# A four-layer RWKV block, two FP4 feed-forward passes and one attention pass on one core: a division seeded from the squared denominator, roots prepared on VectorE, pieces of the normalisations moved to GpSimd, and the FFN weights rounded at the start

## The reference, cut to what matters

```python
y = rwkv(layernorm(x))                  # 4 layers, below
x = x + y
x = x + fp4_ffn(layernorm(x))           # gate, up: 352 columns; silu(gate) * up; down
x = x + causal_attention(layernorm(x))  # inner width 64
x = x + fp4_ffn(layernorm(x))           # the same FFN weights again

# one rwkv layer
h = layernorm(x)*w1 + b1;  hh = h shifted by one token
k, v, r = (h*tm + hh*(1-tm)) @ W.T      # three mixes, three matrices
# scan over tokens with a running maximum pp:
out_t = (e1*aa + e2*v_t) / (e1*bb + e2)
x = x + (sigmoid(r) * out) @ Wo.T
h = layernorm(x)*w2 + b2
kf = square(relu(mix(h) @ Wck.T));  x = x + sigmoid(mix(h) @ Wcr.T) * (kf @ Wcv.T)
```

## Time and profile before

| | us |
|---|---|
| median of 3 runs | 1373.24 (1371.58 to 1373.82) |
| the profiled execution | 1373.36 |
| its span, from first to last instruction | 1372.0 |

### The profile page before, as it was taken

The page is one execution under the profiler, slowest core; times in us unless marked ns, Lnnn a source line. Parts: engine busy times, 40 slices in busy tenths (PEclk is TensorE's granted clock), DMA queues, the critical chain, the costliest instruction groups (busy, mean ns, idle before and its releaser), DMA issues.

```text
span 1372.0 us, 23396 instructions
## 1 busy us (share of the span) xinstructions
PE 1274.4 (93%) x7177; PEld 918.9 (67%) x7177; DVE 1247.3 (91%) x2157; ACT 1238.0 (90%) x2411; POOL 1184.9 (86%) x1413
## 2 busy tenths in 40 slices
PE   3589999999999999999999899998999998999997
PEld 1246666766766766766776567765677786677776
DVE  5889999999999999999999999669999577988995
ACT  5689999999999999999999799877787899999875
POOL 6788999999999999999999999969998556765784
PEclk9789999999999999999999999999999999999999
DMA  7000000001000000000000000100000000000011
GB/s 236 1 0 2 1 1 1 2 1 33 1 1 1 1 1 1 1 1 1 1 1 1 1 2 8 32 23 25 23 1 1 1 1 1 1 16 17 24 31 39
DMA packets 26924, 18.54 MB, mean 14 GB/s; under 512 B 1072, under 2 KB 26160, under 8 KB 26800
## 3 DMA queue, kind: packets, MB, share of 16 engines
q1 hardware_dynamic: 26800, 17.05, 4.2%
HBM read 12.85 MB, written 4.19 MB: 12 GB/s over the span
## 4 chain that ended last, share of the span: by engine, by line
ACT 32%; PE 26%; POOL 17%; issue 14%; DVE 11%; DMA 0%; ACTq 0%; SPq 0%; POOLq 0%; DVEq 0%
ACT z L793 6%; PE ps L1265 4%; ACT kf L913 4%; ACT kf L906 4%; PE ps L1237 3%; PE ps L1244 3%; PE ps L1315 3%; ACT past L898 3%; ACT h L840 2%; POOL W L740 2%; PE ps L1253 2%; PE ps L1297 2%; POOL W L746 2%; PE ps L1080 1%; ACT rc L878 1%
## 5 line engine op out<-in xcount | busy, mean ns | idle before, releaser
L1206 PEld LDWEIGHTS ps<-W,kf 128*128 128x128 f32 x2048 | 248.3, 192 | 58.6 <-issue 58.4
L1188 PE MATMUL ps<-xk,W 128*128 128x512 f32 x512 | 253.6, 598 | 0.8 <-ACT kf L906 0.8
L1206 PE MATMUL ps<-W,kf 128*128 128x128 f32 x2048 | 248.6, 275 | 0.0
L906 ACT ACTIVATE kf<-ps 128x512 f32<-128x512 f32 x256 | 147.1, 599 | 5.4 <-PE ps L1188 5.4
L1080 PEld LDWEIGHTS ps<-idn,z 128*128 128x128 f32 x664 | 78.8, 143 | 104.0 <-issue 53.7
L1080 PE MATMUL ps<-idn,z 128*128 128x128 f32 x664 | 104.6, 281 | 44.7 <-POOL z L651 18.5
L793 ACT ACTIVATE z<-X,ln_rs 128x128 f32<-128x128 f32 x320 | 137.9, 502 | 2.7 <-POOL ln_rs L613 2.6
L913 ACT ACTIVATE kf<-kf 128x1024 f32<-128x1024 f32 x128 | 136.2, 1065 | 0.0
L746 POOL TENSOR_TENSOR W<-W,hsc 128x704 f32<-128x704 f32 x64 | 88.8, 1388 | 47.0 <-DVE W L503 46.8
L1188 PEld LDWEIGHTS ps<-xk,W 128*128 128x128 f32 x512 | 87.1, 192 | 62.4 <-issue 53.9
L611 POOL TENSOR_TENSOR ln_rs<-ln_rs,mhalf 128x8 f32<-128x8 f32 (+1 forms) x70 | 111.1, 1587 | 0.0
(11 more groups left out here) (182 smaller groups left out, 3841.8 us busy)
## 6 DMA issues: line engine op xcount, KB each, us to landing
X<-x_in SPq DMA_DIRECT2D x16, 256.0 KB, 6.6
xi<-x_in SPq DMA_DIRECT2D x16, 256.0 KB, 2.9
out<-X SPq DMA_DIRECT2D x16, 256.0 KB, 2.3
W<-weights SPq DMA_DIRECT2D x4, 832.0 KB, 8.3
W<-fp4w SPq DMA_DIRECT2D x1, 560.0 KB, 3.7
row<-rows SPq DMA_DIRECT2D x1, 192.0 KB, 3.0
wqkv<-qkv SPq DMA_DIRECT2D x1, 96.0 KB, 6.1
idn<-ident SPq DMA_DIRECT2D x1, 64.0 KB, 3.2
```

Of the source, the lines that this page charges most:

```text
L906: e.activation(kf[r % 3][:, f, :], (pF0, pF1)[f % 2][:, :], ACT.Relu).then_inc(relu_done[f], 1)
L1188: e.matmul((pF0, pF1)[f % 2][:, :], w_of(r, WCK + f), xk[r % 2][:, :], start=True, stop=True).then_inc(kf_mm[f], 1)
L1206: last = e.matmul(chunk(pKV, j), kf[r % 3][:, f, j * 128:(j + 1) * 128], w_of(r, WCV + f), start=f == 0 and j == 0, stop=f == 3, skip_grou ...
```

## The change

The division: the seed is now computed from den squared (one more ACT operation, `Square`, into `rc`, and a wait of ACT on itself, `den2_done`), with half the slope. The end is one square and one DVE operation in place of two; `mul_u` is gone, and signs and constants are folded into `WO`.

`w` is added to d already in `sub_d` (one DVE operation as before, of another kind), so that both `Relu` of `args` and the clip need no bias tile; the constants of the clip are adapted.

`rsqrts` on POOL keeps the power and the product. The two operations before it are made by DVE in a new step `variances`, on the same 128x8 tiles.

Norm 1 is now 2 + 2 pieces, norm 2 is 1 + 3 (ACT + POOL): POOL does 5 of 8 where it did 3 of 8.

The FFN weights are loaded right after the fourth tile of x, into the space of layer 1, and rounded in ticks 1 to 5; PE transposes them in ticks 10 to 12, in three steps, ACT copies them in ticks 7 to 9, and the attention matrices are folded at the start. SP issues the loads of layers 1 to 3 behind a wait for the last transposition; `PREPARE_AT` moves DVE's scaling of those layers to ticks 12, 18 and 26.

All four order lists are rewritten, with other offsets.

```diff
-SEED = LN2 * (127.0 - 0.04367744889921346)
-CUBIC, LEAD = 0.9991106956842978, 1.000889996847986
+SEED = LN2 * 0.5 * (127.0 - 0.048852061236122075)
+VERTEX, REST, LEAD = 1.4972871244454433, 0.7471212163971999, 1.0056154043227372
...
+            def variances(s):
+                if 0 <= s < NR + LN2_LAG:
...
+                    e.tensor_scalar(rs[:, 1, :], st[:, :, 1], -1.0, None, ALU.mult)
+                    e.tensor_scalar(rs[:, 2, :], st[:, :, 2], 1.0 / 128.0, EPS, ALU.mult, ALU.add).then_inc(ready, 1)
...
             def sub_d(r):
-                    e.tensor_tensor(dd[r % 2][:, :], pK[:, :], pp[r % 2][:, 0:T], ALU.subtract).then_inc(d_done, 1)
+                    e.scalar_tensor_tensor(out=dd[r % 2][:, :], in0=pK[:, :], scalar=col(ew, r), in1=pp[r % 2][:, 0:T],
+                                           op0=ALU.add, op1=ALU.subtract).then_inc(d_done, 1)
...
-            def mul_u(r):
-                if 0 <= r < NR:
-                    w.wait_ge(sq1_done, r + 1)
-                    w.wait_ge(ps_done, r + 1)
-                    e.scalar_tensor_tensor(out=pO[:, :], in0=pO[:, :], scalar=CUBIC, in1=p[r % 2][:, :],
-                                           op0=ALU.add, op1=ALU.mult).then_inc(u_done, 1)
...
             def rwkv(r):
-                    w.wait_ge(u_done, r + 1)
-                    e.scalar_tensor_tensor(out=rc[r % 2][:, :], in0=er[r % 2][:, :], scalar=2.0, in1=pO[:, :],
-                                           op0=ALU.subtract, op1=ALU.mult).then_inc(rwkv_done, 1)
+                    w.wait_ge(sq1_done, r + 1)
+                    w.wait_ge(ps_done, r + 1)
+                    e.scalar_tensor_tensor(out=rc[r % 2][:, :], in0=pO[:, :], scalar=REST, in1=p[r % 2][:, :],
+                                           op0=ALU.add, op1=ALU.mult).then_inc(rwkv_done, 1)
...
             def rsqrts(s):
-                    roots(n_1.rs2[s % 3][:, :, lo:hi], n_1.st2[s % 3][:, lo:hi, :], n_1.nr)
+                    w.wait_ge(ready, s + 1)
+                    e.tensor_tensor(rs[:, 0, :], rs[:, 2, :], mhalf[:, 0:hi - lo], ALU.pow).then_inc(*own.next())
+                    w.wait_ge(*own.so_far())
+                    e.tensor_tensor(rs[:, 1, :], rs[:, 1, :], rs[:, 0, :], ALU.mult).then_inc(n_1.nr, 1)
...
-                    e.activation(ed[r % 2][:, 0, :], dd[r % 2][:, :], ACT.Relu, bias=col(ew, r))
-                    e.activation(ed[r % 2][:, 1, :], dd[r % 2][:, :], ACT.Relu, bias=col(wneg, r), scale=-1.0).then_inc(args_done, 1)
+                    e.activation(ed[r % 2][:, 0, :], dd[r % 2][:, :], ACT.Relu)
+                    e.activation(ed[r % 2][:, 1, :], dd[r % 2][:, :], ACT.Relu, scale=-1.0).then_inc(args_done, 1)
...
             def seeds(r):
                 if 0 <= r < NR:
                     w.wait_ge(wo_mm, r - 1)
                     w.wait_ge(den_done, r + 1)
-                    e.activation(rc[r % 2][:, :], er[r % 2][:, :].bitcast(I32), ACT.Exp, bias=SEED,
-                                 scale=-LN2 / 2.0 ** 23).then_inc(seed_done, 1)
+                    e.activation(rc[r % 2][:, :], er[r % 2][:, :], ACT.Square).then_inc(den2_done, 1)
+                    w.wait_ge(den2_done, r + 1)
+                    e.activation(rc[r % 2][:, :], rc[r % 2][:, :].bitcast(I32), ACT.Exp, bias=SEED,
+                                 scale=-LN2 / 2.0 ** 24).then_inc(seed_done, 1)
...
+                if b == 3:
+                    e.dma_start(qw, fp4w).then_inc(fp4_here, 16)
+            w.wait_ge(q_turned, 3)
+            for l in range(1, L):
+                e.dma_start(W[:, l, :], weights[:, l, :]).then_inc(w_here[l], 16)
```

More of the change, by code:

```diff
@@ L570, in vector @@
-                a_bn(att_job(t - 1))
-                f_bn(ffn_job(t + 2))
-                scan_pp(t - 4)
                 a_inverse(att_job(t - 5))
-                a_add(att_job(t - 6))
-                mul_u(t - 6)
-                fx_add(ffn_job(t - 2))
+                rwkv(t - 6)
+                sub_d(t - 4)
                 mul_up(ffn_job(t - 4), 0)
                 mul_up(ffn_job(t - 4), 1)
+                bn2(t - 7)
                 fx_sub(ffn_job(t - 2))
+                fx_scale(ffn_job(t - 1))
@@ L580, in vector @@
+                fh_add(ffn_job(t - 5), 0)
+                mix_k(t - 8)
+                mix_r(t - 8)
+                mul_up(ffn_job(t - 4), 2)
                 gated(t - 5)
-                sub_d(t - 4)
-                fh_add(ffn_job(t - 5), 0)
-                mul_up(ffn_job(t - 4), 2)
-                rwkv(t - 6)
                 fh_sub(ffn_job(t - 5), 0)
-                fx_scale(ffn_job(t - 1))
                 mul_up(ffn_job(t - 4), 3)
-                bn2(t - 7)
+                variances(t - 1)
@@ new lines, in vector @@
+                init_stats(t + 2)
+                a_mask(att_job(t - 4), 1)
+                prepare(t)
+                bn1(t)
+                mul_rv(t - 4)
+                fx_max(ffn_job(t))
+                a_max(att_job(t - 4), 1)
+                mul_s1(t - 4)
+                add_xa(t - 6)
+                weights_scales(t - 1)
+                scan_bb(t - 4)
+                a_mask(att_job(t - 4), 2)
+                scan_aa(t - 4)
+                a_max(att_job(t - 4), 2)
+                a_mask(att_job(t - 4), 3)
@@ L870, in exp_r @@
                 if 0 <= r < NR:
+                    w.wait_ge(vecs_done, VECS)
                     w.wait_ge(argr_done, r + 1)
-                    e.activation(er[r % 2][:, :], er[r % 2][:, :], ACT.Exp, bias=v_of(r, TF)).then_inc(er_done, 1)
+                    e.activation(er[r % 2][:, :], er[r % 2][:, :], ACT.Exp, bias=col(now, r)).then_inc(er_done, 1)
             def seeds(r):
@@ L884, in square_1 @@
                     w.wait_ge(y_done, r + 1)
-                    e.activation(pO[:, :], er[r % 2][:, :], ACT.Square, bias=-1.0).then_inc(sq1_done, 1)
+                    e.activation(pO[:, :], er[r % 2][:, :], ACT.Square, bias=-VERTEX).then_inc(sq1_done, 1)
             def norm2(r):
@@ new lines, in tensor @@
+                a_values(att_job(t - 8))
+                a_keys(att_job(t - 7))
+                weights_turned(t - 12, 2)
+                p_turn(att_job(t - 9), 2)
+                similarity(att_job(t - 8), 2)
+                p_turn(att_job(t - 9), 3)
+                values(t - 8)
+                similarity(att_job(t - 8), 3)
+                a_turn(att_job(t - 6))
+                turn1(t - 6)
+                ff_values(t - 14, 1)
+                keys(t - 7)
+                h_turn(ffn_job(t - 10), 2)
@@ L1367, in sync @@
+                f_gate(ffn_job(t - 7), 3)
+                f_up(ffn_job(t - 7), 2)
         def sync():
```

362 lines of the change are left out of this document (169 added, 193 removed).

## The result

| | before | after |
|---|---|---|
| median of 4 runs (us) | 1372.41 (1371.47 to 1373.82) | 1359.19 (1354.47 to 1361.77) |
| the profiled execution | 1373.36 | 1361.77 |
| its span | 1372.0 | 1360.5 |

The ratio is 0.990 (95% interval 0.987 to 0.993): 13.2 us less, where 31.5 were forecast. The forecast's own range (1332 to 1352) doesn't hold 1359; the range of all (1326 to 1362) does, because it was drawn to take in rival A.

The account below looks back on a forecast made before the run. Four engines stood within 3%, only DVE never resting; afterwards ACT would bound at 12.5 us a tick. Savings of 14.0, 8.0, 4, 1.5 and 4 sum to 31.5 off 1373.4: 1342 us (own range 1332 to 1352, all 1326 to 1362).

Parts of the forecast that it names:

- rival A: DVE-POOL lock where norm 1's pieces and the power meet variances or mixes: period stays 12.78 us, 1356 us total; chance 0.22.
- The steady tick: Jobs 13 to 63: period falls from 12.78 to 12.50 us, -14.0 us over 50 periods (-21.5 to 0).
- Every wait is met: Walk of the new lists around one steady tick: waits between engines have 0.3 to 1.5 us to spare.
- the rounding: FFN weight rounding leaves jobs 55 to 58 (-8.0 us) for ticks 1 to 5, where half hides (+4).
- B: Same lock, POOL a phase later: the first mix waits 1.26 us every tick, period 13.61, 1397 us; chance 0.08.
- the ties of POOL's phase: Argument against the slower rival: POOL waits for variances, and rwkv waits for POOL 1.6 us later.
- One reading of the prediction: Earlier trace: POOL's L651 lasts 1.95 instead of 0.88 us, to just after L288's end at 767.69, as evidence of the lock.
- DVE's 12.35: DVE's own work a steady tick: 12.78 less 0.59 for mul_u plus 0.16 for variances, the period's lower bound.
- The wait for its own result: ACT's seed Exp waits for its Square: 0.19 us a tick (0 to 0.71), beside 0.52 for the Square.
- Jobs 7 to 13 and the fill: First jobs: -4 us net for the fill (-12 to +6), -1.5 us for jobs 7 to 13 (-3 to 0).
- The border: Before the FFN: PE's 4.04 us of weight transposition and folding moves to ticks 10 to 12, -4 us (-6 to 0).
- rival C: New order loses outside the steady stretch: fill +6 instead of -4, FFN and attention ticks +10, 1362 us; chance 0.08.

Follow-up runs that it names:

- e5: Against the kernel after: first_past is made by DVE behind mix_r instead of by POOL; 1350.28 us, ratio 0.984.
- e6: Against the kernel after: first_past on DVE, and norm1_rest ahead of arg_r in POOL's list; 1345.62 us, ratio 0.981.
- e2: Against the kernel after: first_past issued for all 64 jobs at its place on POOL, not just a layer's first two; 1409.84 us, ratio 1.028.
- e8: Against the kernel after: the two operations of variances go back from DVE to POOL, in front of the power; 1426.16 us, ratio 1.039.
- e10: Against e6: the division of before, with the seed from den, no Square or its wait on ACT, mul_u back on DVE; 1378.92 us, ratio 1.005.
- e7: Against the kernel after: the FFN weights are not rounded but used as loaded; 1353.56 us, ratio 0.986.

## Why the prediction was wrong

**The steady tick: the sums right, the step "Every wait is met" wrong.** The period of the quick ticks is 12.53 where 12.50 was forecast, and e5 and e6 show it over all 50 jobs: 626.6 and 626.9 us, where 50 x 12.50 is 625. The kernel after takes 643.43, so it saves 3.6 us there instead of the forecast 22 (14.0 for the period and 8.0 for the rounding). The walk through the lists that found "between 0.3 and 1.5 us to spare" looked at waits on semaphores. It did not give the lock between DVE and POOL a state of its own, and it walked one ordinary tick, not that of a border. The pieces of norm 1 end 0.07 us behind the first mix's start in the quick tick: there was no slack at all where the lock matters. Of the 18.4 us that the forecast has too much here, 16.6 are the slow jobs and 1.5 the 0.03 us a tick.

**POOL.** The forecast was 12.04 us; it is 12.30 in a quick tick, where the power lasts 2.07 us beside the mixes and not the 1.67 of before. In a late tick it is 13.4: the two pieces of norm 1, priced at 0.44 each, then take 1.2 each. This, with the lock left out of the walk, is the term that failed.

**Rival A was the right mechanism at the wrong place and size.** It had `variances` and the first mix against two pieces and the power. Its signs were a first mix over 0.8 us or a power over 1.9, and its 537 us for 42 jobs and 1356 in all are close to the 538.35 measured from job 13 to 55 and to 1359. That is luck. A spread the loss over every tick, 0.28 us each. In truth most ticks lose only 0.03 against the forecast and 19 lose 0.5 to 1.0; the power over 1.9 us (2.07) is the sign of the quick ticks, and the first mix is 0.74 in both ticks shown and over 0.8 in only 8 of the 51 jobs from 13 on. The loss sits in the pieces, which three mixes hold off, and comes back to DVE by way of PE and ACT. B, the slower rival, had the late phase as a state of its own, with POOL a phase later and 13.61 us a job in every tick. But its price was wrong in its kind: it let the first mix wait 1.26 us for POOL, and in the late ticks it is POOL that waits. It was argued away by the ties of POOL's phase. The ties hold in one direction only: POOL waits for `variances` if early (0.18 us in e6), but nothing pulls it forward when it is late. e2 and e8 stay in the late phase from job 13 on, at 13.7 to 14.3 us a job, and are slower than before.

One reading of the prediction was off: after L288 (until 767.69) POOL's two pieces L651 end not just behind it but at 768.46, 0.77 us later, so nearly all of their 0.88 lay behind it. That speaks for the lock more clearly than the prediction said.

The Trainium skill states the lock as a rule ("SBUF — State Buffer", section "SBUF: two separate sides"): whoever starts first holds the pair of ports for the whole instruction. The slow ticks agree in that the mixes hold off the pieces (2.44 us against 0.91), and the tick of job 26 in that the pieces hold off the mixes (0.94 against 0.74). Who comes first the starts of the rows don't tell: pieces that start 0.02 to 0.07 us ahead of the first mix mostly lost to it. For the power the trace shows more than the page: it waits 0.4 us (2.07 against 1.65), yet the second mix (from 616.11) and the third (from 616.77) run their usual 0.74 us inside its time, which ends at 617.70.

**DVE's own work.** Two terms were mis-sized, 0.18 us in sum. `sub_d` as a kind with a per-partition scalar takes 612.60 - 611.94 = 0.66 us from start to start, not the 0.59 of the kind of `mul_u` in the earlier trace rows. `variances` costs 615.45 - 615.18 = 0.27 in the quick tick, not 0.16; the second of the two lasts until the piece of norm has ended (615.54 and 615.52), and e10 has 0.15 without that piece. In e6 `arg_r` is beside it in the same way: 519.06 - 518.75 = 0.31. So DVE's 12.35 is 12.53 and is the bound, in place of ACT.

**ACT.** The wait for its own result: 513.70 - 513.04 = 0.66 us between the starts of `Square` and `Exp`, where neighbours without a wait are 0.52 apart, so the new operation and its wait come to 0.52 + 0.14; forecast 0.52 + 0.19. ACT's tick is 297.48 / 300 of 12.54 = 12.43 us in e6, against 12.53.

**Jobs 7 to 13 and the fill.** Up to the d of job 13 the kernel gained 205.52 - 201.68 = 3.8 us, forecast 4 + 1.5. The rounding was forecast at +4 and costs 4 to 5 (e7). The removed loops give 7 or 8: without rounding the d of job 7 comes 118.61 - 110.39 = 8.2 us earlier. The d of job 0 is later (32.33 against 29.51) and that of job 7 at 115.47, forecast 114.

**The border and the rest.** From the d of job 63 (before: 852.54) to the end of the span the time went from 519.5 to 515.4 us, -4.1, forecast -4. From the last `add_xb` on it is 453.5 against 452.6: the FFN and attention ticks with their new order neither gained nor lost (PE is busy 49.72 of 50 us there, against 49.07 in the earlier trace rows), as forecast, and rival C fell.

In sum: -3.6 - 3.8 - 4.1 = -11.5 us of span, against a forecast of 31.5, of which the steady part misses 18 us. With the slow jobs gone, as in e6, the change gives 27.2 us.

**What stays open.** Two groups of slow jobs are seen to end with the pieces first and DVE waiting (jobs 26 and 39), the third (job 61) ends without such a tick, and why they last 4 jobs or 8 isn't shown: a start 0.06 us ahead lost at job 23 and won at job 39. In e2 the late phase never ends. The runs of one program differ by 7 us, which fits groups of differing length, but only one run of each has a trace.

## What to carry to other kernels

With four engines within 3% of each other, adding up an engine's own work gives the period only if the order is stable: list, for each operation of GpSimd beside VectorE operations with two SBUF inputs, how far it is from meeting them, and what a small delay does. If the late phase makes the late engine the bound, it can hold itself for several jobs, and a 0.2 us operation at two jobs of a layer decides 0.7% of the time (e5). The cure was cheap here: the rare operation on the other engine, and the pieces one step earlier, 13.6 us together (e6). And two edits that relieve two engines at the same bound are to be priced together; either alone was worth nothing here.

## What the runs showed of the hardware

Between VectorE operations with two SBUF inputs, back to back and 0.66 us apart, GpSimd does get a turn, but not at each gap. Two pieces that started 0.02 us ahead of three mixes took 1.58 and 0.87 us, or 0.96 and 1.37, where 0.45 is usual: 2.3 to 2.4 us in place of 0.91, with one piece let in behind the first or second mix and the other behind the third. The mixes hardly felt it (0.74 to 0.79 us). When the pieces won, at job 26, the first two mixes paid 0.2 us each.

The tiny operation on 128x2 elements was held the same way, 0.72 us against 0.19, and so was VectorE's on 128x8: at 512.97 it lasted 0.55, to the end of GpSimd's `arg_r` (513.48), against 0.16 alone. Small operations had no privilege here: they waited as long as their neighbour lasted. The power, long for its 8 elements (1.65 us), is the exception that fits beside mixes: 2.07 us there, at no cost to them.
